# Moving the projection of k's second half ahead of a group of transposes in step 3

## The chip, the cores and the metric

The kernel runs on one core of one Trainium2 chip. The metric is the device time of one execution in microseconds (us). A time given below is the median of several runs; the profile is of one further execution.

## The reference

Attention over x [4, 1024, 128] with 16 heads of 64, then a layer norm, a feed-forward part with a token shift, and a second layer norm. Cut to what matters here:

```python
q = (x @ Wq).reshape(B, N, H, Dh).transpose(0, 2, 1, 3)      # B=4, N=1024, H=16, Dh=64
kv = x @ Wkv                                                 # k and v likewise
s = jnp.einsum('bhid,bhjd->bhij', q * scale, k)
gm = jnp.max(s, axis=-1, keepdims=True)
p = jnp.where(causal_mask, 0.0, jnp.exp(s - gm))
out = jnp.einsum('bhij,bhjd->bhid', p, v) / (jnp.sum(p, axis=-1, keepdims=True) + EPS)
x = _layernorm(x + (out.transpose(0, 2, 1, 3).reshape(B, N, H * Dh) @ Wo + bo))
x = _layernorm(x + ffn(x))
```

## The kernel before

The heads go through in 32 pairs `p` (4 batches of 8 pairs), two heads `a` = 0, 1 at a time. A pair has 8 steps `t`, one for each query tile of 128 rows. The order of the work on each engine is written out by hand, one loop over `p` and `t` for each engine (TensorE from L1114, ScalarE from L626, VectorE from L838, GpSimd from L434, the DMA queue of SyncE from L354); semaphores join them.

A query tile goes through the engines like this:

- TensorE, `scores(p, t)` (L974, its matmuls are recorded at L984): 12 matmuls fill two of three score buffers `ps_s`, one for each head. They wait until VectorE has emptied the buffers used before.
- VectorE, `evacuate(p, t, a)` (L746): scales a score buffer by -1/8 into an SBUF slot `tile` and takes the row minimum. For query tiles 4 to 7 VectorE also transposes blockwise (L755).
- GpSimd, `mask(p, t, a)` (L407): the diagonal block of 128x128.
- ScalarE, `exp_of(p, t, a)` (L576): the exponential over (t+1)*128 columns with its row sum.
- For query tiles 0 to 3 TensorE transposes the exponentials (`turn_tile`, L989, recorded at L997) one or more steps later, into a shared PSUM bank, and ScalarE copies them out to `pt` (`take_turned`, L610, recorded at L624). Tiles 2 and 3 are turned one head at a time, as `TURNED_IN` says: head 0 is part 0, head 1 is part 1.

Beside this TensorE does other work in each step: the projections of v (L927) and of the next pair's q and k (`qk_of`, L1001, recorded at L918; a projection is 3 matmuls of 512 columns, and ScalarE copies it out in `take_qk`, L579, recorded at L584, into `x1t` or `full`), the product with v (`values`, L1038), and the output projection (`project_out`, L1049). `QK` lists the four halves q 0, q 1, k 0, k 1; half n is projected in step n, so that k's second half is projected in step 3. GpSimd splits each half into a high and a low part (`split`, L391, recorded at L399 and L401) in step 0, 2, 4 or 5 (`SPLIT_AT`); that of k's second half is in step 5.

All this other work and the transposes share two PSUM banks, `ps_x`. `users_of_banks` (L81) lists the users of the banks in the order in which TensorE comes to them; user number n takes bank n % 2, and `drained` (L952) makes TensorE wait until ScalarE has emptied what user n - 2 had left in that bank.

`TURN_AT` says in which step which query tile is turned: tile 2 in step 3, tile 3 in step 4. `TURN_FIRST` lists the steps in which part 0 of the transposes stands directly behind the scores. In the other steps it stands behind the projections, together with the rest. The set is read in `users_of_banks`, in TensorE's loop and in ScalarE's loop:

```python
TURNED_IN = {0: ((0, 1),), 1: ((0, 1),), 2: ((0,), (1,)), 3: ((0,), (1,))}
TURN_AT = {1: 0, 2: 1, 3: 2, 4: 3}
TURN_FIRST = (1, 3, 4)
```

In the last pair, where no next pair is left to project, `turn_half` (L1060, recorded at L1066) and `take_sums` (L519, recorded at L522) take the place of `qk_of` and `take_qk`. Where a batch's x is turned for the next batch (pairs 1, 2, 9, 10, 17 and 18, `x_half`), step 1 has four more transposes and ScalarE two more copies.

Of the kernel before, what the change touches and what calls it, by code (L numbers as in the profile page):

```python
# [45 lines left out]
SPLIT_AT = {0: 0, 2: 1, 4: 2, 5: 3}  # L46
V_AT = {0: 0, 1: 1}
TURN_AT = {1: 0, 2: 1, 3: 2, 4: 3}
TURN_FIRST = (1, 3, 4)
X_AT = 1  # L50
OUT1_AT = 2
OUT0_AT = 4
# [28 lines left out]
def users_of_banks(p, t):  # L81
    users = []
    turned = [("quad", p, TURN_AT[t], n) for n in range(len(TURNED_IN[TURN_AT[t]]))
              ] if t in TURN_AT and p < ALL_PAIRS else []
    if t in TURN_FIRST:
        users += turned[0:1]
# [6 lines left out]
    if t == OUT1_AT and 1 < p:  # L93
        users.append(("out", p - 2, 1))
    users += turned[1:] if t in TURN_FIRST else turned
    if t == OUT0_AT and 0 < p <= ALL_PAIRS:
# [24 lines left out]
def build(nc, x, wq, wkv, wo, bo, w_r, w_k, w_v, mu_r, mu_k, out):  # L121
    r_dram = nc.dram_tensor("recips", [2, 2, N], F32).ap()

    with ExitStack() as ctx:  # L124
# [348 lines left out]
        def _(act):  # L473
# [121 lines left out]
            def take_values(p, k):  # L595

                c = min(k, 1)
                lo, hi = ((0, HALF), (HALF, HALF + 2 * P), (HALF + 2 * P, N))[k]
                act.wait_ge(s_pv[k], p + 1)

                at_least(act, s_yadd[c], p)
                act.activation(ot[:, lo:hi], ps_x[BANK["pv", p, k]][:, lo - c * HALF:hi - c * HALF], ACT.Copy
                               ).then_inc(s_ot[k], 1)

            def take_out(p, c):
                act.wait_ge(s_out, 2 * p + c + 1)
                act.activation(ot[:, c * HALF:(c + 1) * HALF], ps_x[BANK["out", p, c]][:, :], ACT.Copy  # L607
                               ).then_inc(s_outc, 1)

            def take_turned(p, t, n):  # L610
                heads = TURNED_IN[t][n]
                bank = ps_x[BANK["quad", p, t, n]][:, :]

                at_least(act, s_pv[0], p)
                act.wait_ge(s_quad, 8 * p + 2 * t + heads[-1] + 1)
                if t == 0:
                    act.activation(pt_unit(0).rearrange("p a (x c) -> p x a c", x=2)[:, :, :, 0:32],
                                   bank[:, 0:2 * P].rearrange("p (x a i) -> p x a i", x=2, a=4), ACT.Copy
                                   ).then_inc(s_pt, 1)
                    return  # L620
                for m, a in enumerate(heads):
                    cols = bank[:, m * (t + 1) * P:(m + 1) * (t + 1) * P].rearrange("p (j a i) -> p j a i", a=4, i=32)
                    place = pt_unit(t // 2)[:, :, place_of(t, a)].rearrange("p a (j i) -> p j a i", i=32)
                    act.activation(place, cols, ACT.Copy).then_inc(s_pt, 1)  # L624

            for p in range(ALL_PAIRS):  # L626
                for t in range(TILES):
# [4 lines left out]
                    if t == 7 and p > 0:  # L632
                        take_values(p - 1, 1)
                    if t in TURN_FIRST:
                        take_turned(p, TURN_AT[t], 0)
# [6 lines left out]
                    if t == OUT1_AT and p > 1:  # L642
                        take_out(p - 2, 1)
                    if t in TURN_AT and t not in TURN_FIRST:
                        take_turned(p, TURN_AT[t], 0)
# [263 lines left out]
        def _(pe):  # L909
# [64 lines left out]
            def scores(p, t):  # L974
                if t == 0 and p > 0:
                    pe.wait_ge(s_qklo, 4 * p)
                if p == 0 and t == 0:
                    pe.wait_ge(s_xy, 2)
                at_least(pe, s_evac, SLOTS * p + 2 * t + 2 - NSCORES)
                for c in range(2):  # L980
                    for m, (kh, qh) in enumerate(terms):
                        for a in range(2):
                            rows = slice(a * DH, (a + 1) * DH)
                            ins = mm(ps_s[scores_at(p, t, a)][:, c * HALF:(c + 1) * HALF], qs[rows, p % 2, qh, t * P:(t + 1) * P],  # L984
                                     ks[rows, p % 2, kh, c * HALF:(c + 1) * HALF], start=(m == 0), stop=(m == 2))
                            if c == 1 and m == 2:
                                ins.then_inc(s_scores, 1)

            def turn_tile(p, t, n):  # L989
                unit = ("quad", p, t, n)  # L990
                heads = TURNED_IN[t][n]
                drained(unit)
                for m, a in enumerate(heads):
                    pe.wait_ge(s_exp, SLOTS * p + 2 * t + a + 1)
                    for j in range(t + 1):
                        at = (m * (t + 1) + j) * P
                        ins = turn(ps_x[BANK[unit]][:, at:at + P], tile[:, slot_of(p, t, a), j * P:(j + 1) * P],  # L997
                                   ident[:, :])
                    ins.then_inc(s_quad, 1)
# [114 lines left out]
            for p in range(ALL_PAIRS):  # L1114
                for t in range(TILES):
                    scores(p, t)
                    if t in TURN_FIRST:
                        turn_tile(p, TURN_AT[t], 0)
# [8 lines left out]
                    if t in TURN_AT:  # L1127
                        for n in range(1 if t in TURN_FIRST else 0, len(TURNED_IN[TURN_AT[t]])):
                            turn_tile(p, TURN_AT[t], n)
# [75 lines left out]
```

## Time and profile before

| | |
|---|---|
| time, median of 3 runs | 1093.92 us (1092.81 to 1093.97) |
| the profiled execution's own time | 1094.0 us |
| its span, first to last instruction | 1092.0 us |
| TensorE busy | 1033.6 us (95%) |
| VectorE busy | 915.4 us (84%) |
| ScalarE busy | 746.6 us (68%) |
| GpSimd busy | 582.3 us (53%) |
| mean granted TensorE clock | 0.993 |

PE is TensorE's matmul row, PEld its weight loads, DVE is VectorE, ACT ScalarE, POOL GpSimd. Busy time of PE is of pipelined matmuls whose ends are modelled, so that one instruction can begin before the recorded end of the one before it. In a row of the timeline "x3" is three instructions merged, and "[0.31 <-ACT pt L624]" says that the engine was idle for 0.31 us before it and that the end of this wait came from ScalarE's instruction of line 624. ACT and DVE instructions also overlap a little: the next one begins about 0.1 us before the recorded end of the one before.

### The profile page before, as it was taken

The page shows a single profiled execution, that of the slowest core. Times are in us where ns is not written, and L with a number is a line of the kernel's source. Part 1 is how long each engine was busy: PE and PEld are TensorE (multiplying, and loading weights), DVE is VectorE, ACT ScalarE, POOL GpSimd, SP SyncE. Part 2 cuts the span into 40 slices and gives each one's busy share as a digit, 9 for nine tenths or more (in the row PEclk, how much of TensorE's full clock was granted, in tenths as well). Part 3 has the DMA queues.
Part 4 walks back from the last instruction along what each step waited for, and adds up shares of the span by engine and source line. Part 5 has one row for each costly group of instructions (what it writes and reads, how often), then busy time and mean ns, then how long its engine had stood idle before and what let it go on. Part 6 is the DMA issues. An engine that isn't in the chain of part 4 may idle for free. (4 is left out here: it accounts for less than half of the span.)

```text
span 1092.0 us, 22065 instructions
## 1 busy us (share of the span) xinstructions
PE 1033.6 (95%) x7427; PEld 673.6 (62%) x7427; DVE 915.4 (84%) x1546; ACT 746.6 (68%) x1709; POOL 582.3 (53%) x918
## 2 busy tenths in 40 slices
PE   7799999999999999999999999999999999999895
PEld 5565666666665666666666666666666666666563
DVE  5888888888887988888888888889888888898957
ACT  5766666666666666676666666666666766766767
POOL 5345655555564556566544556655555565554354
PEclk9999999999999999999999999999999999999998
DMA  5245555445555445555644455564445556554442
GB/s 162 69 111 123 136 141 123 117 111 125 134 124 136 118 109 122 131 123 136 146 113 106 114 134 123 139 145 118 115 114 126 132 126 146 123 124 117 115 106 77
DMA packets 74208, 134.05 MB, mean 123 GB/s; under 512 B 26864, under 2 KB 36848, under 8 KB 74096
## 3 DMA queue, kind: packets, MB, share of 16 engines
q1 hardware_dynamic: 73520, 132.26, 51.0%
q8 instruction: 59, 0.97, 0.4%
q10 hardware_dynamic: 576, 0.39, 0.1%
q14 instruction: 53, 0.43, 0.1%
HBM read 21.17 MB, written 2.36 MB: 22 GB/s over the span
## 5 line engine op out<-in xcount | busy, mean ns | idle before, releaser
L746 DVE TENSOR_SCALAR_CACHE_REDUCE tile<-ps_s 128x1024 f32<-128x1024 f32 x512 | 608.1, 1222 | 135.6 <-PE ps_s L984 128.0
L576 ACT ACTIVATE tile<-tile,neg_max 128x640 f32<-128x640 f32 (+7 forms) x512 | 396.2, 774 | 213.3 <-POOL tile L407 213.2
L984 PE MATMUL ps_s<-ks,qs 64*128 64x512 f32 x3072 | 424.2, 408 | 10.4 <-DVE tile L746 9.2
L407 POOL TENSOR_SCALAR_AFFINE_SELECT tile<-tile 128x128 f32<-128x128 f32 x512 | 149.7, 293 | 456.1 <-DVE tile L746 454.3
L984 PEld LDWEIGHTS ps_s<-ks,qs 64*128 64x128 f32 x3072 | 268.7, 184 | 129.3 <-issue 59.6
L1038 PE MATMUL ps_x<-pt,vs 128*64 128x256 f32 (+1 forms) x2560 | 270.2, 362 | 0.0
L755 DVE STREAM_TRANSPOSE stage<-tile 128x640 f32<-128x640 f32 (+3 forms) x256 | 255.2, 1026 | 0.0
L1038 PEld LDWEIGHTS ps_x<-pt,vs 128*64 128x64 f32 x2560 | 173.1, 137 | 109.3 <-issue 35.4
L997 PE MATMUL ps_x<-ident,tile 128*128 128x128 f32 x640 | 117.4, 290 | 26.5 <-ACT pt L624 15.8
L997 PEld LDWEIGHTS ps_x<-ident,tile 128*128 128x128 f32 x640 | 69.0, 140 | 107.0 <-issue 51.5
L918 PE MATMUL ps_x<-xs,ws 128*128 128x512 f32 x381 | 119.4, 423 | 0.6 <-DVE xs L721 0.4
L415 POOL TENSOR_TENSOR ot<-ot,rb 128x512 f32<-128x512 f32 x64 | 104.0, 1626 | 7.8 <-issue 5.2
L624 ACT ACTIVATE pt<-ps_x 128x256 f32<-128x256 f32 (+2 forms) x192 | 89.2, 483 | 12.3 <-PE ps_x L997 12.3
L576 ACT ACTIVATION_READ_ACCUMULATOR tile<-tile,neg_max 128x1 f32 x512 | 96.8, 189 | 0.0
L422 POOL TENSOR_TENSOR y<-y,ot 128x512 f32<-128x512 f32 x64 | 83.1, 1299 | 7.4 <-ACT ot L607 7.4
L401 POOL TENSOR_TENSOR qs<-x1t,qs 128x512 fp32r<-128x512 f32 x62 | 79.2, 1278 | 5.3
L591 ACT ACTIVATE vs<-ps_x 128x512 f32<-128x512 f32 x64 | 38.3, 598 | 56.5 <-PE ps_x L927 56.5
L918 PEld LDWEIGHTS ps_x<-xs,ws 128*128 128x128 f32 x381 | 63.5, 192 | 19.5 <-issue 11.3
L1049 PE MATMUL ps_x<-ot,wos 128*128 128x512 f32 x128 | 68.1, 613 | 2.8 <-POOL ot L415 2.4
L584 ACT ACTIVATE x1t<-ps_x 128x512 f32<-128x512 f32 x93 | 55.5, 597 | 9.3 <-PE ps_x L918 6.2
L927 PE MATMUL ps_x<-ws,xs 128*128 128x256 f32 x384 | 61.8, 296 | 0.0
L927 PEld LDWEIGHTS ps_x<-ws,xs 128*128 128x128 f32 x384 | 51.2, 193 | 11.5 <-issue 11.2
(92 smaller groups left out, 579.2 us busy)
## 6 DMA issues: line engine op xcount, KB each, us to landing
pt<-stage SPq DMA_DIRECT2D x512, 120.0 KB, 2.4
pt<-stage SPq DMA_DIRECT2D x512, 88.0 KB, 2.1
rb<-recips SPq DMA_DIRECT2D x64, 256.0 KB, 4.0
y<-in_L_attn_x SPq DMA_DIRECT2D x3, 512.0 KB, 8.7
out<-y SPq DMA_DIRECT2D x3, 512.0 KB, 3.2
pt<-in_L_attn_Wkv SPq DMA_DIRECT2D x2, 384.0 KB, 6.8
pt<-in_L_attn_x SPq DMA_DIRECT2D x2, 256.0 KB, 4.5
wos<-in_L_attn_Wo SPq DMA_DIRECT2D x1, 512.0 KB, 7.1
```

Source lines behind the costliest of these rows:

```text
L407: pool.affine_select(out=block_of, in_=block_of, compare_op=ALU.is_ge, fill=fill, base=0, pattern=[[-1, P]], channel_multiplier=1).then_in ...
L415: pool.tensor_tensor(cols, cols, rb[:, :].rearrange("p (i t) -> p t i", t=TILES)[:, 4 * c:4 * c + 4, :], ALU.mult).then_inc(s_norm[c], 1)
L422: pool.tensor_tensor(cols, cols, ot[:, c * HALF:(c + 1) * HALF], ALU.add).then_inc(s_yadd[c], 1)
L576: act.activation(cols, cols, ACT.Exp, bias=neg_max[:, at:at + 1], scale=-1.0, accum_out=sums[:, p % 2, a, t:t + 1]).then_inc(s_exp, 1)
L624: act.activation(place, cols, ACT.Copy).then_inc(s_pt, 1)
L746: dve.tensor_scalar(tile[:, at, :], ps_s[scores_at(p, t, a)][:, :], -SCALE, None, ALU.mult, ALU.min, accum_out=neg_max[:, at:at + 1]).then ...
L755: dve.transpose(stage_unit(u)[:, :, place_of(t, a)], tile[:, slot_of(p, t, a), 0:(t + 1) * P].rearrange("p (j b k) -> p b j k", b=4, k=32) ...
L918: ins = mm(bank, ws[:, "qk".index(what), wh, r * P:(r + 1) * P], xs[:, b % XSLOTS, xh, c * HALF:(c + 1) * HALF], start=(m == 0), stop=(m = ...
L927: ins = mm(bank[:, 2 * t * P:2 * (t + 1) * P], xs[:, b % XSLOTS, xh, at], ws[:, 2, wh, r * P:(r + 2) * P], start=(m == 0), stop=(m == 2))
L984: ins = mm(ps_s[scores_at(p, t, a)][:, c * HALF:(c + 1) * HALF], qs[rows, p % 2, qh, t * P:(t + 1) * P], ks[rows, p % 2, kh, c * HALF:(c + ...
L997: ins = turn(ps_x[BANK[unit]][:, at:at + P], tile[:, slot_of(p, t, a), j * P:(j + 1) * P], ident[:, :])
L1038: ins = mm(bank[a * DH:(a + 1) * DH, cols + (j == final) * P:cols + 2 * P], vs[:, v_place(p // 2, j), p % 2, a * DH:(a + 1) * DH], moving, ...
```

## The change

One entry of `TURN_FIRST` goes. It has three effects, all in step 3 of every pair:

- TensorE: the order scores, transposes of tile 2 head 0, projection of k's second half, transposes of tile 2 head 1 becomes scores, projection, transposes of head 0, transposes of head 1.
- ScalarE: `take_turned` of tile 2 head 0, `take_qk` of k's second half, `exp_of(p, 3, 0)` becomes `take_qk`, `take_turned`, `exp_of(p, 3, 0)`. The copy of head 1 stays between `exp_of(p, 3, 0)` and `exp_of(p, 3, 1)`.
- Banks: the three users of step 3 change places in the list, so that the projection gets the bank that head 0's transposes had, head 0's transposes get the other one, and head 1's transposes stay in their bank. That bank's user before them is now the projection; before the change it was head 0's transposes.

```diff
--- before.py
+++ after.py
@@ -46,7 +46,7 @@
 SPLIT_AT = {0: 0, 2: 1, 4: 2, 5: 3}
 V_AT = {0: 0, 1: 1}
 TURN_AT = {1: 0, 2: 1, 3: 2, 4: 3}
-TURN_FIRST = (1, 3, 4)
+TURN_FIRST = (1, 4)
 X_AT = 1
 OUT1_AT = 2
 OUT0_AT = 4
```

## Rows read from the trace of the kernel before

**Rows 1.** The page: busy time of TensorE, and the granted clock in 40 slices.

```profile
PE 1033.6 (95%) x7427; PEld 673.6 (62%) x7427; DVE 915.4 (84%) x1546; ACT 746.6 (68%) x1709; POOL 582.3 (53%) x918
PEclk9999999999999999999999999999999999999998
```

**Rows 2.** Waits of PE, 100 to 1000 us: total us, times, longest.

```profile
PE ps_x L997 <- ACT pt L624: 12.7, 28, 1.1
PE ps_x L997 <- ACT tile L576: 9.5, 28, 0.4
```

**Rows 3.** Timeline of PE in an ordinary pair: start us, us, engine line op.

```profile
404.91 0.96 PE L918 MATMUL ps_x<-xs,ws 128*128 128x512 f32 x3
...
405.71 1.02 PE L1049 MATMUL ps_x<-ot,wos 128*128 128x512 f32 x2
...
407.15 1.66 PE L984 MATMUL ps_s<-ks,qs 64*128 64x512 f32 x12
...
408.74 0.55 PE L997 MATMUL ps_x<-ident,tile 128*128 128x128 f32 x3
...
409.04 0.94 PE L918 MATMUL ps_x<-xs,ws 128*128 128x512 f32 x3
...
410.30 0.55 PE L997 MATMUL ps_x<-ident,tile 128*128 128x128 f32 x3 [0.31 <-ACT pt L624]
...
412.37 0.66 PE L997 MATMUL ps_x<-ident,tile 128*128 128x128 f32 x4
...
413.36 0.63 PE L997 MATMUL ps_x<-ident,tile 128*128 128x128 f32 x4 [0.33 <-ACT tile L576]
```

**Rows 4.** Timeline of ACT in the same pair.

```profile
407.32 0.66 ACT L624 ACTIVATE pt<-ps_x 128x256 f32<-128x256 f32 x2
...
409.16 0.62 ACT L576 ACTIVATE tile<-tile,neg_max 128x384 f32<-128x384 f32 x1 [0.59 <-POOL tile L407]
...
409.68 0.18 ACT L576 ACTIVATION_READ_ACCUMULATOR tile<-tile,neg_max 128x1 f32 x1
...
409.77 0.47 ACT L624 ACTIVATE pt<-ps_x 128x384 f32<-128x384 f32 x1
...
410.14 0.59 ACT L584 ACTIVATE x1t<-ps_x 128x512 f32<-128x512 f32 x1
...
411.32 0.73 ACT L576 ACTIVATE tile<-tile,neg_max 128x512 f32<-128x512 f32 x1 [0.58 <-POOL tile L407]
...
412.04 0.47 ACT L624 ACTIVATE pt<-ps_x 128x384 f32<-128x384 f32 x1
...
412.41 0.71 ACT L576 ACTIVATE tile<-tile,neg_max 128x512 f32<-128x512 f32 x1
```

**Rows 5.** Timeline of DVE and POOL in the same pair.

```profile
407.53 1.22 DVE L746 TENSOR_SCALAR_CACHE_REDUCE tile<-ps_s 128x1024 f32<-128x1024 f32 x1
...
409.77 1.27 POOL L401 TENSOR_TENSOR qs<-x1t,qs 128x512 fp32r<-128x512 f32 x1
...
410.99 0.69 POOL L407 TENSOR_SCALAR_AFFINE_SELECT tile<-tile 128x128 f32<-128x128 f32 x2
...
412.56 1.22 DVE L746 TENSOR_SCALAR_CACHE_REDUCE tile<-ps_s 128x1024 f32<-128x1024 f32 x1 [1.25 <-PE ps_s L984]
...
416.68 1.23 DVE L746 TENSOR_SCALAR_CACHE_REDUCE tile<-ps_s 128x1024 f32<-128x1024 f32 x1 [1.74 <-PE ps_s L984]
```

**Rows 6.** Timeline of PE in pair 0, a pair that turns x, and the last pair.

```profile
25.78 0.55 PE L997 MATMUL ps_x<-ident,tile 128*128 128x128 f32 x3
...
26.91 0.55 PE L997 MATMUL ps_x<-ident,tile 128*128 128x128 f32 x3
...
29.89 0.63 PE L997 MATMUL ps_x<-ident,tile 128*128 128x128 f32 x4 [0.26 <-ACT tile L576]
...
314.07 0.55 PE L997 MATMUL ps_x<-ident,tile 128*128 128x128 f32 x3 [1.07 <-ACT pt L624]
...
1011.66 0.55 PE L997 MATMUL ps_x<-ident,tile 128*128 128x128 f32 x3 [0.95 <-ACT pt L624]
```

## The prediction

> **What bounds the kernel now.** I read the page first. TensorE is busy for 95% of the span and its granted clock is full in nearly every slice [rows 1], so the question is where its remaining idle time lies and what closes each gap. The list of TensorE's waits answers: over 28 pairs nearly all its idle time is two waits a pair, both ahead of transposes [rows 2]. One ends with ScalarE's copy of line 624, 12.7 us in 28 waits; the other ends with an exponential, 9.5 us in 28 waits, or 0.34 us each, with a longest one of 0.4.
>
> The timeline of an ordinary pair, by engine, shows which these are. TensorE runs scores of step 3 at 407.15, head 0's transposes of tile 2 at 408.74, the projection at 409.04, and then stands still until 410.30, when head 1's transposes of tile 2 begin; scores of step 4 and head 0's transposes of tile 3 (412.37) follow; it stands still again until 413.36 [rows 3]. What the reader is to see is that TensorE is not what sets the second start. Followed back: head 1's transposes of tile 3 (413.36) need its exponential, begun at 412.41. That stood in ScalarE's queue behind the copy of 412.04, this behind the exponential of 411.32, and this waited for GpSimd's mask [rows 4]. The mask (410.99) came as soon as GpSimd was through with the subtraction of 409.77, which had begun behind the mask of tile 2 and so goes back to VectorE's pass of 407.53 [rows 5]. From the scores of step 2 to 413.36 the chain runs over VectorE, GpSimd and ScalarE, and the first gap of TensorE is slack within it. From 413.36 on TensorE is again the one that all wait for: VectorE stands idle for 1.74 us before it can begin step 5 [rows 5].
>
> **What the change removes.** The wait of head 1's transposes for the copy of head 0's goes, since they no longer follow each other in one bank. No instruction is added or taken away, no shape changes, and the moved work issues no DMA; it is moved past nothing on SyncE's queue or GpSimd's.
>
> **What it adds.** Head 1's transposes now wait for `take_qk` of the same step. I work out when each thing happens in the ordinary pair.
>
> 1. The projection starts where head 0's transposes did, at 408.74. Its bank was last used by an output projection, copied out before the copies of 407.32. Three projection matmuls hold TensorE for 405.71 - 404.91 = 0.80 us before the next group starts, and end after 0.96 us by the record [rows 3]. So it ends at 408.74 + 0.96 = 409.70.
> 2. Head 0's transposes start at 408.74 + 0.80 = 409.54. Their bank was emptied by the two copies of tile 1 (407.32 + 0.66 = 407.98), and ScalarE has begun head 1's exponential at 409.16, so head 0's is done [rows 4]. No new wait. They hold TensorE for 409.04 - 408.74 = 0.30 us, until 409.84, and end at 409.54 + 0.55 = 410.09 [rows 3].
> 3. ScalarE is free at 409.77, as before: that is when it began the copy behind the exponential [rows 4]. The projection is there since 409.70, so `take_qk` runs 409.77 to 410.36 (0.59 us). The copy of head 0's transposes follows after 0.5 us, 410.27 to 410.74, its input being ready at 410.09. Both together take ScalarE as long as in the old order, and both lie ahead of the exponential of 411.32, which has 0.58 us of idle time before it [rows 4].
> 4. Head 1's transposes start when `take_qk` is out. Before, the copy ended at 409.77 + 0.47 = 410.24 and they started at 410.30, 0.06 later [rows 3, 4]. Now it is 410.36 + 0.06 = 410.42. So the wait is not gone: it ends 0.59 - 0.47 = 0.12 us later.
> 5. Scores of step 4 and head 0's transposes of tile 3 slide by these 0.12 us, from 412.37 to 412.49. Head 1's of tile 3 have an idle time of 0.33 us before them [rows 3], and the exponential that ends it comes by a chain in which nothing has moved: VectorE's pass, GpSimd's mask and subtraction, ScalarE's exponential, the copy of head 1 (ready at 410.42 + 0.55 = 410.97, wanted at 412.04) and the next exponential [rows 4, 5]. The idle time shrinks to 0.21 us and the start stays at 413.36. VectorE begins step 4 (412.56) 0.12 us later and takes this out of the 1.74 us for which it waits before step 5 [rows 5].
>
> Sum for an ordinary pair: +0.12 us off the path, 0.00 on it. The six pairs that turn x have a first gap of 1.07 us, not 0.31 [rows 6], because the exponential is later; the difference of the two copies is the same 0.12 us, and the second gap is 0.34 there as elsewhere (28 waits, longest 0.4) [rows 2]. So zero too.
>
> Pair 0 is different: head 1's transposes did not wait there (26.91). Now they would start at 25.78 + 0.96 (projection) + 0.05 + 0.59 (copy) + 0.06 = 27.44, 0.53 us later, against a second gap of 0.26 us [rows 6]; some 0.3 us may remain of which the transposes' modelled ends hide a part. I take 0.1, with 0 and 0.5 as bounds, once. In the last pair a copy of sums takes the projection's place (wait of 0.95 us before the transposes [rows 6]); 0.12 us at most, once, and I take 0.
>
> Total: 31 x 0.00 + 0.1 = +0.1 us. The profiled execution took 1094.0 us (span 1092.0), 0.1 above the median of 1093.92, so I forecast 1094.0 us against that median.
>
> **A rule weighed.** The two groups of tile 2's transposes shared one bank before, and head 1's waited for head 0's copy [rows 3]; after the change they lie in different banks. The Trainium skill, Perfetto Trace Analysis, section Optimizing Tensor Performance, wants independent matmul groups rotated through different PSUM banks so that the evacuation of one overlaps the matmuls of the next; by that rule this order should be the better one and the first wait should go. By the sum above it doesn't go, since the bank that head 1's transposes get was filled just before by the projection, and the copy of that stands behind the same exponential.
>
> **The rivals.**
>
> - **The 0.12 us are paid in every pair (slower).** The place is the second gap. It decides once head 1's transposes of tile 2 come more than the 0.33 us later that the gap holds. My 0.12 leaves 0.21 spare, but step 3 above has ScalarE free only 0.07 us behind the projection's end: were the projection 0.3 us slower at the head of its new place than in step 2, the gap would be used up. If the slack were not there at all the price is 0.12 x 31 = 3.7 us, 1097.7 us. Against it: all 28 second gaps are alike (0.34 on average, longest 0.4) [rows 2], and each is an idle time recorded behind a modelled end, so the true slack is no smaller. 10%.
> - **The first wait really goes (faster).** This is the rotation rule as a mechanism: head 1's transposes start as soon as TensorE gets there (409.84) or its exponential is read out (409.68 + 0.18 = 409.86 [rows 4]), and the first gap closes. Were TensorE's own stream the bound throughout, that would be 31 gaps: 25 of some 0.33 and six of 1.07, about 14.7 us, or 1079.3 us. For it speaks that these are real idle times of the busiest engine. Against it: `take_qk` stands in the queue behind the same exponential, and even with the gap closed the chain over GpSimd sets 413.36. 3%.
> - **A small gain elsewhere (faster).** The projection is out 0.3 us earlier and its consumer, the split of step 5, could start earlier. It stands in GpSimd's queue at a time set by the masks of step 5, long after. At most what the second gap shows, if the exponential came earlier: 31 x 0.34 = 10.5 us, 1083.5 us; nothing moves it. 3%.
> - **Nothing changes on the path**, my forecast: 84%.
>
> **How the numbers follow.** 0.2% of 1093.9 is 2.2 us, about what a measurement of this kernel can tell from no change. The forecast (+0.1 with bounds 0 and +0.6 for pairs 0 and last) lies within it; so does half of the slower rival's span. The range reaches from 1092.4, the runs' own spread below the median, to 1096.0, up to which the slower rival is held in part. Faster 0.06, same 0.84, slower 0.10.
>
> **What the profile after would show.** Right: TensorE in step 3 has scores, L918, two groups of L997, and the wait of the second group ends with ScalarE's L584 and no longer L624. It is recorded from the modelled end of head 0's transposes (410.09), so it reads 410.42 - 410.09 = 0.33 us where it read 0.31. The wait for L576 shrinks from 0.34 to about 0.21 each; the time from one pair to the next stays as it was. Wrong, slower: the wait for L576 vanishes and the pair grows. Wrong, faster: no wait before the second group, and the exponential of step 3, head 1, earlier relative to the scores of step 2. The forecast also fails if ScalarE, GpSimd or VectorE have other durations once their neighbours in time move, which no row here prices.

## The result and the profile after

The changed kernel takes 1097.66 us (median of 5 runs, 1096.97 to 1098.53), the kernel before 1093.92 us beside it (5 runs, 1092.81 to 1094.25). The ratio is 1.004, with a 95% interval of 1.0029 to 1.0052. The change makes the kernel 0.4% slower. I had forecast no change and a range up to 1096.0.

The page of the changed kernel shows the same number of instructions and the same clock. TensorE's busy time is 6.6 us longer than in [rows 1] and ScalarE's 5.1 us, so the loss is recorded as work and not as waiting (the ends of matmuls are modelled, and the first experiment below, with the same order and a shorter copy, has 1034.8 us):

```profile
span 1096.5 us, 22065 instructions
PE 1040.2 (95%) x7427; PEld 678.6 (62%) x7427; DVE 914.0 (83%) x1546; ACT 751.7 (69%) x1709; POOL 582.3 (53%) x918
PEclk9999999999999999999999999999999999999998
```

TensorE's waits between 100 and 1000 us in the changed kernel, to be held against [rows 2]:

```profile
PE ps_x L997 <- ACT x1t L584: 14.1, 28, 1.1
PE ps_x L997 <- ACT tile L576: 6.4, 28, 0.2
```

Both lines are what the prediction had said. The first wait has not gone; it now ends with the copy of k's half (L584). The second has shrunk from 0.34 us each to 6.4 / 28 = 0.23. By this list TensorE waits less in all than before (20.5 us against 22.2), and yet the kernel is slower.

From pair 1 on the loss comes evenly. Here is the start of head 1's transposes of tile 3 in pairs 1 and 30 (PE's timeline), first in the kernel before:

```profile
61.54 0.63 PE L997 MATMUL ps_x<-ident,tile 128*128 128x128 f32 x4 [0.35 <-ACT tile L576]
...
983.52 0.63 PE L997 MATMUL ps_x<-ident,tile 128*128 128x128 f32 x4 [0.34 <-ACT tile L576]
```

and in the changed one:

```profile
62.27 0.63 PE L997 MATMUL ps_x<-ident,tile 128*128 128x128 f32 x4 [0.23 <-ACT tile L576]
...
988.00 0.63 PE L997 MATMUL ps_x<-ident,tile 128*128 128x128 f32 x4 [0.24 <-ACT tile L576]
```

The distance grows from 0.73 to 4.48 us: 3.75 us in 29 pairs, 0.13 us a pair. That is the size of the 0.12 us that I had worked out for the later start and then called hidden. The 0.73 us that are there in pair 1 are looked at below.

An ordinary pair of the changed kernel, TensorE (PE) and its weight loads (PEld), from the scores of step 3 on, answers to [rows 3]:

```profile
409.30 1.66 PE L984 MATMUL ps_s<-ks,qs 64*128 64x512 f32 x12
...
410.89 0.98 PE L918 MATMUL ps_x<-xs,ws 128*128 128x512 f32 x3
...
411.71 0.49 PE L997 MATMUL ps_x<-ident,tile 128*128 128x128 f32 x3
...
412.56 0.55 PE L997 MATMUL ps_x<-ident,tile 128*128 128x128 f32 x3 [0.36 <-ACT x1t L584]
...
414.63 0.66 PE L997 MATMUL ps_x<-ident,tile 128*128 128x128 f32 x4
...
415.51 0.63 PE L997 MATMUL ps_x<-ident,tile 128*128 128x128 f32 x4 [0.22 <-ACT tile L576]
...
416.10 0.30 PEld L1049 LDWEIGHTS ps_x<-ot,wos 128*128 128x128 f32 x2 [0.20 <-issue]
416.13 1.10 PE L1049 MATMUL ps_x<-ot,wos 128*128 128x512 f32 x2
```

and its ScalarE, which answers to [rows 4]:

```profile
411.92 0.59 ACT L584 ACTIVATE x1t<-ps_x 128x512 f32<-128x512 f32 x1
...
412.40 0.49 ACT L624 ACTIVATE pt<-ps_x 128x384 f32<-128x384 f32 x1
...
415.18 0.19 ACT L576 ACTIVATION_READ_ACCUMULATOR tile<-tile,neg_max 128x1 f32 x1
...
415.38 0.60 ACT L624 ACTIVATE pt<-ps_x 128x512 f32<-128x512 f32 x1
```

The same place in the kernel before, with rows that stand in no group so far:

```profile
413.02 0.19 ACT L576 ACTIVATION_READ_ACCUMULATOR tile<-tile,neg_max 128x1 f32 x1
413.12 0.60 ACT L624 ACTIVATE pt<-ps_x 128x512 f32<-128x512 f32 x1
...
413.83 0.30 PEld L1049 LDWEIGHTS ps_x<-ot,wos 128*128 128x128 f32 x2
413.87 1.10 PE L1049 MATMUL ps_x<-ot,wos 128*128 128x512 f32 x2
```

Counted from the start of the scores of step 3 (407.15 and 409.30):

| | before | after |
|---|---|---|
| head 1's transposes of tile 2 start | 3.15 | 3.26 |
| head 0's transposes of tile 3 start, end | 5.22, 5.88 | 5.33, 5.99 |
| head 1's transposes of tile 3 start | 6.21 | 6.21 |
| ScalarE's copy of head 0's (L624) starts, ends | 5.97, 6.57 | 6.08, 6.68 |
| output projection: weight load starts | 6.68 | 6.80 |

The third row is the one that I had taken for the end of the matter: it has not moved. The instruction behind it has. The output projection (L1049) lies in the bank in which head 0's transposes of tile 3 lie, and waits for their copy. That copy started 0.09 us after the recorded end of the transposes in both kernels, so it went along with them, and the weight load followed 0.11 to 0.12 us behind the copy in both.

Pair 0 has no output projection in step 4, and pays more, once. The scores of steps 3 and 5 and VectorE's first pass of step 4 in the kernel before:

```profile
24.20 1.65 PE L984 MATMUL ps_s<-ks,qs 64*128 64x512 f32 x12
...
29.17 1.22 DVE L746 TENSOR_SCALAR_CACHE_REDUCE tile<-ps_s 128x1024 f32<-128x1024 f32 x1 [0.81 <-PE ps_s L984]
...
30.46 1.66 PE L984 MATMUL ps_s<-ks,qs 64*128 64x512 f32 x12
```

and in the changed one, with head 1's transposes of tile 2:

```profile
24.28 1.66 PE L984 MATMUL ps_s<-ks,qs 64*128 64x512 f32 x12
...
27.52 0.55 PE L997 MATMUL ps_x<-ident,tile 128*128 128x128 f32 x3 [0.36 <-ACT x1t L584]
...
29.79 1.23 DVE L746 TENSOR_SCALAR_CACHE_REDUCE tile<-ps_s 128x1024 f32<-128x1024 f32 x1 [1.35 <-PE ps_s L984]
...
31.07 1.66 PE L984 MATMUL ps_s<-ks,qs 64*128 64x512 f32 x12 [0.39 <-DVE tile L746]
```

Step 3 begins 0.08 us later in the changed kernel. Counted from there, head 1's transposes start at 3.24 us in place of 2.71 (26.91 in [rows 6]), 0.53 later, and the scores of step 5 at 6.79 in place of 6.26, again 0.53 later. They stand 0.05 to 0.07 us behind the end of VectorE's pass in both kernels: in this pair the whole delay goes on over VectorE. With the 0.08 us this is 0.61 of the 0.73 us by which the traces differ in pair 1; the other 0.12 come up between 42 and 51 us, and what they are stays open. So the price is about 0.5 us for pair 0 and 0.12 us for each of the 31 others.

### The profile page after: what moved, and what is told of

The parts are those of the page before. It is cut to its first block and busy times, and to the rows that moved or that the text cites. A ratio compares the mean times of both kernels' runs of the same rounds, so it can differ in the third digit from the quotient of the medians.

```text
span 1096.5 us, 22065 instructions
## 1 busy us (share of the span) xinstructions
PE 1040.2 (95%) x7427; PEld 678.6 (62%) x7427; DVE 914.0 (83%) x1546; ACT 751.7 (69%) x1709; POOL 582.3 (53%) x918
## 5 line engine op out<-in xcount | busy, mean ns | idle before, releaser
L1038 PE MATMUL ps_x<-pt,vs 128*64 128x256 f32 (+1 forms) x2560 | 270.2, 362 | 0.0
L1038 PEld LDWEIGHTS ps_x<-pt,vs 128*64 128x64 f32 x2560 | 173.0, 137 | 109.4 <-issue 35.5
L997 PEld LDWEIGHTS ps_x<-ident,tile 128*128 128x128 f32 x640 | 71.5, 140 | 92.7 <-issue 37.1
L624 ACT ACTIVATE pt<-ps_x 128x256 f32<-128x256 f32 (+2 forms) x192 | 89.9, 487 | 9.5 <-PE ps_x L997 9.1
L1049 PE MATMUL ps_x<-ot,wos 128*128 128x512 f32 x128 | 67.9, 612 | 2.7 <-POOL ot L415 2.3
L584 ACT ACTIVATE x1t<-ps_x 128x512 f32<-128x512 f32 x93 | 55.4, 596 | 9.5 <-PE ps_x L918 6.4
```

The source lines that it names most:

```text
L1038: ins = mm(bank[a * DH:(a + 1) * DH, cols + (j == final) * P:cols + 2 * P], vs[:, v_place(p // 2, j), p % 2, a * DH:(a + 1) * DH], moving, ...
```

## The experiments

All were run beside the kernel before on the same chip; each ratio is against it. For each trace I also give the length of a pair that turns x (from one start of the 32 matmuls of L1038 in step 7 to the next, median of five): 33.39 us before, 33.52 after. The other pairs are shorter (31.43 and 31.56) and differ by as much. Theory A is the chain over the bank. Theory B is that the order costs TensorE itself something. Theory C is that the delay reaches the path another way than over that bank.

### Undo the longer copy, keep the new order

```diff
-                act.activation(full[n], ps_x[BANK["qk", p, n]][:, :], ACT.Copy).then_inc(s_full, 1)
+                cols = 384 if n == 3 else HALF
+                act.activation(full[n][:, 0:cols], ps_x[BANK["qk", p, n]][:, 0:cols], ACT.Copy).then_inc(s_full, 1)
```

> The changed kernel, with ScalarE copying only 384 of the 512 columns of k's second half out of PSUM (128 columns of k are left stale), so that this copy is as short as the 384-column copy for which head 1's transposes waited before. Theory A (a chain over a bank): the longer copy makes head 1's transposes of tile 2 start 0.12 us later, this makes head 0's transposes of tile 3 end 0.12 us later, ScalarE's copy of those too, and the output projection of step 4, whose bank that copy empties, starts later by as much in every pair. Then the 0.12 us go and the time is that of the kernel before, 1093.9 (+-0.7). Theory B (order on TensorE): to have the projection between the scores and the transposes costs TensorE itself something, by weight loads or by the switch of shapes. Then the time stays at 1097.7.

Measured: 1093.89 us against 1092.84, ratio 1.0008 (0.9999 to 1.0017); pair 33.40 us. From pair 1 on the loss is gone, though TensorE still has the new order and the new banks. Theory B falls: what the change costs there is the length of the copy that head 1's transposes wait for. In pair 0 the product with v still comes 8.28 us after the scores of step 3 (24.48 and 32.76), 0.44 later than before: there head 1's transposes did not wait at all, and now they wait until the projection is done and copied, however short the copy.

### Shorten the copy that empties the output projection's bank

```diff
+                    few = 3 if p > 0 and (t, n) == (3, 0) else t + 1
-                    act.activation(place, cols, ACT.Copy).then_inc(s_pt, 1)
+                    act.activation(place[:, 0:few], cols[:, 0:few], ACT.Copy).then_inc(s_pt, 1)
```

> The changed kernel, with ScalarE copying only three of the four blocks of head 0's transposes of tile 3 in step 4 (one block of the transposed exponentials is left stale from pair 1 on), which ends that copy about 0.12 us sooner. Theory A: the output projection gets its bank 0.12 us sooner and the whole loss comes back: 1093.9 to 1094.5. Theory B: the time stays near 1097.7. A third theory C (the 0.12 us reach the path over the exponential of step 3 or over VectorE, not over the bank): stays near 1097.7 too, while the short copy of k would still recover it.

Measured: 1094.3 us against 1092.84, ratio 1.001 (1.0001 to 1.0019); pair 33.40 us. Most of the loss is back, by an edit that leaves everything up to the transposes of tile 3 as in the changed kernel. It begins with pair 1, so the 0.5 us of pair 0 stay. Its rows of step 4:

```profile
413.49 0.65 PE L998 MATMUL ps_x<-ident,tile 128*128 128x128 f32 x4
...
414.24 0.49 ACT L625 ACTIVATE pt<-ps_x 128x384 f32<-128x384 f32 x1
...
414.84 0.30 PEld L1050 LDWEIGHTS ps_x<-ot,wos 128*128 128x128 f32 x2
```

The copy still starts late (0.10 us behind the transposes' end), ends at 414.73 thanks to its shorter length, and the weight load comes 0.11 us behind it.

### The same in the kernel before

The same edit on the kernel before.

> The kernel before, with the same shortened copy of head 0's transposes of tile 3. In the trace of before TensorE starts the output projection 0.51 us after head 1's transposes, as close as four transposes allow (0.49 us elsewhere), so the copy and TensorE's own stream end almost together. Theory A: at most 0.02 to 0.05 us a pair to gain, 1092.3 to 1093.9. If instead the bank is a wait of its own size in the kernel before too, the gain would be near 0.12 us a pair, 1090.2.

Measured: 1089.49 us against 1092.84, ratio 0.9971 (0.996 to 0.9981); pair 33.28 us. My expectation was a miss: 0.11 us a pair came back, not 0.02 to 0.05. So the kernel before was already waiting for that bank in every pair. Its rows:

```profile
412.49 0.49 ACT L625 ACTIVATE pt<-ps_x 128x384 f32<-128x384 f32 x1
...
413.10 0.30 PEld L1050 LDWEIGHTS ps_x<-ot,wos 128*128 128x128 f32 x2
```

The weight load again comes 0.12 us behind the copy's end (412.98). Held against the run above, which has the same short copy, the change of step 3 still costs 0.12 us a pair (33.40 against 33.28): both wait for that copy, and with the new order it starts later by what its transposes come later. In the kernel before, the wait stands in no list, because the four transposes ahead of the projection are recorded until 413.36 + 0.63 = 413.99, after the projection has begun. The Trainium skill, Perfetto Trace Analysis, Tensor Engine Instruction, says that TensorE's recorded ends are estimated from size and delay and not observed; this case agrees, with a wait of 0.1 us beneath a recorded overlap.

### Delay the copy in the kernel before, with no change of order

```diff
             for p in range(ALL_PAIRS):
                 for t in range(TILES):
+                    if t == 3:
+                        act.activation(pad_to[:, :], bo_col[:, :], ACT.Copy)
```

> The kernel before with one more ScalarE instruction in each pair, a copy of one column between SBUF tiles, right ahead of the copy of head 0's transposes of tile 2. TensorE's order, the banks and everything else stay as before. By the nearest rows (the accumulator read holds ScalarE for 0.09 us net, an 8-column activation for about 0.2) it delays that copy by 0.1 to 0.25 us. Theory A: this delay alone does what the change did, 31 x 0.1 to 0.25 = 3 to 8 us slower, 1097 to 1102. Theory B: the time stays at 1093.9, for nothing of TensorE's order has changed.

Measured: 1095.7 us against 1092.84, ratio 1.0025 (1.0016 to 1.0034); pair 33.49 us. The rows:

```profile
410.96 0.19 ACT L630 ACTIVATE pad_to<-bo_col 128x1 f32<-128x1 f32 x1
411.06 0.47 ACT L625 ACTIVATE pt<-ps_x 128x384 f32<-128x384 f32 x1
```

The copy starts 0.10 us later than it would have, and the pair is 0.10 us longer. The time lies below the 1097 to 1102 that I had expected, since the kernel beside it took 1092.84 and the delay was the least of those that I had allowed for; 2.9 us against 31 x 0.10 = 3.1 fits. The old order with a later copy does what the change did, in the same proportion.

### Is it a slope or a point?

The changed kernel with 256 columns (the first diff with `cols = 256`), and the changed kernel with the added instruction of the last diff.

> The changed kernel, with ScalarE copying only 256 of the 512 columns of k's second half (half of it is left stale), so that head 1's transposes of tile 2 can start some 0.1 us earlier than in the kernel before. Theory A, refined by the rows so far: in the kernel before, ScalarE is free for the copy of head 0's transposes of tile 3 at the same moment, to 0.01 us, at which their result is there. A delay costs one for one and an advance gains nothing: the time is that of the run with 384 columns, 1093.9, and not 3 us below it. Rival D: the time is proportional on both sides, and this run comes to about 1090.5.

> The changed kernel with the one-column ScalarE copy in front of the copy of k's second half, the instruction that cost the kernel before 2.7 us (0.10 us a pair at its place). Theory A: past the point at which ScalarE and the transposes meet, every delay counts in full: 0.10 x 31 = 3.1 us more than the changed kernel, 1100 to 1101. A rival in which 0.12 us is a step of its own (another order of waiting, once) and not a slope: about 1098.

Measured: 1093.11 us against 1093.13 with 256 columns, ratio 0.9996 (0.9987 to 1.0005), pair 33.39; 1099.45 us against 1093.43 with the added instruction, ratio 1.0052 (1.004 to 1.0064), pair 33.59. The second lies a little under the 1100 to 1101 that I had expected. The first kernel starts head 1's transposes of tile 2 at 3.04 us, 0.11 earlier than before (410.71 - 407.67), and its rows show why nothing is gained:

```profile
412.81 0.63 PE L998 MATMUL ps_x<-ident,tile 128*128 128x128 f32 x4
...
413.55 0.19 ACT L576 ACTIVATION_READ_ACCUMULATOR tile<-tile,neg_max 128x1 f32 x1
413.64 0.59 ACT L625 ACTIVATE pt<-ps_x 128x512 f32<-128x512 f32 x1
```

The transposes end at 413.44, 0.20 us before the copy starts, and what it waits for is ScalarE's own exponential. Earlier is worth nothing, later costs in full up to nearly twice the delay of the change: 33.39, 33.52 and 33.59 us a pair for a start of head 1's transposes of tile 2 that is 0, 0.11 and 0.20 us later than before. The kernel before stands at the bend, to 0.01 us (an instruction begins 0.09 to 0.10 us ahead of the recorded end of a readout, so ScalarE is free at 413.02 + 0.19 - 0.09 = 413.12, or 5.97 after the scores; the transposes' result is there at 5.88 + 0.09 = 5.97).

### Take the output projection away from the bank

First out of step 4, with `OUT0_AT = 5` in place of 4, in both kernels. The bank is the same there, but its copy has long been out when the projection comes.

> The changed kernel with the output projection of the previous pair moved from step 4 to step 5, behind the scores. It no longer stands behind the copy that empties its bank. Theory A: the change of order in step 3 then costs nothing, and this run and its twin (the kernel before with the same move) have the same time within 1 us; both about 1091 to 1093, since TensorE keeps the same work and loses only a few hundredths of a us at the seams. Theory B or C: this run is 3 to 4 us slower than its twin.

> The kernel before with the output projection of the previous pair moved from step 4 to step 5: the twin of the run above. Theory A: same time as that, about 1091 to 1093. Theory B or C: 3 to 4 us faster than that.

Measured: 1097.25 us on the changed kernel (1.0033, 1.002 to 1.0046), 1095.86 us on the kernel before (1.0023, 1.0014 to 1.0032), against 1093.13; pairs 33.52 and 33.48 us. The difference of the twins fell from 3.7 us to 1.4, but not to the 1 us or less that I had expected, and both are slower than the kernel before, where I had expected 1091 to 1093. The rows of the changed kernel with the move:

```profile
415.20 1.22 DVE L746 TENSOR_SCALAR_CACHE_REDUCE tile<-ps_s 128x1024 f32<-128x1024 f32 x1 [1.36 <-PE ps_s L984]
...
416.49 1.22 PEld L984 LDWEIGHTS ps_s<-ks,qs 64*128 64x128 f32 x12 [0.21 <-DVE tile L746]
```

With the projection gone, the scores of step 5 stand directly behind the transposes, and these need a third score buffer, which VectorE empties in its first pass of step 4. That pass starts when the scores of step 4 are done, so it too is 0.1 us later in the changed kernel: a second way for the same delay, the one of pair 0. It costs here what it delays the scores of step 5 by, 6.80 us after those of step 3 against 6.77 in the twin. The output projection covers it in its old place (there the scores of step 5 come 1 us later). Why the twin is 2.7 us slower than the kernel before stays open: from the start of head 1's transposes of tile 3 to the product with v (L1038) it takes 3.20 us where that takes 3.12.

Then between the two groups of transposes of tile 3, in both kernels, on TensorE, ScalarE and in the order of banks:

```diff
+    if t == OUT0_AT and 0 < p <= ALL_PAIRS:
+        users.append(("out", p - 1, 0))
     users += turned[1:] if t in TURN_FIRST else turned
-    if t == OUT0_AT and 0 < p <= ALL_PAIRS:
-        users.append(("out", p - 1, 0))
...
+                    if t == OUT0_AT and 0 < p:
+                        take_out(p - 1, 0)
                     if t == 4:
                         take_turned(p, TURN_AT[t], 1)
                     exp_of(p, t, 0)
...
-                    if t == OUT0_AT and 0 < p:
-                        take_out(p - 1, 0)
                     exp_of(p, t, 1)
...
+                    if t == OUT0_AT and 0 < p:
+                        project_out(p - 1, 0)
                     if t in TURN_AT:
                         for n in range(1 if t in TURN_FIRST else 0, len(TURNED_IN[TURN_AT[t]])):
                             turn_tile(p, TURN_AT[t], n)
-                    if t == OUT0_AT and 0 < p:
-                        project_out(p - 1, 0)
```

> The kernel before with the output projection of step 4 put between the two groups of transposes of tile 3, on TensorE, on ScalarE (its copy ahead of head 1's) and in the order of the banks. It fills TensorE's wait for the exponential of head 1. Its bank is then that which the copy of tile 2 head 1 empties, which is done 0.8 us before; head 1's transposes wait for the copy of head 0's instead, some 0.47 us later than now, but scores of step 5 follow them directly. Theory A: 0.4 to 0.48 us a pair gained, 1079 to 1082. Rival: ScalarE, which now has to copy two things in turn before the exponential of step 4, delays that by about 0.9 us and eats the gain: 1090 or more.

> The changed kernel with the output projection of step 4 between the two groups of transposes of tile 3, the same move as in the run of the kernel before that took 1088.7 us. There the projection no longer waits for the copy of head 0's transposes but for GpSimd's product that is its operand, at 6.14 us after the scores of step 3; head 1's transposes start behind it at 7.10, and their bank is free from 6.67. With the 0.12 us that the change adds the bank would be free at 6.79, still 0.3 ahead of 7.10. Theory A: here the change of step 3 costs nothing, 1088.7 (+-1). Theory C (the 0.12 us reach the path another way than over that bank): 1092.4, which is 3.7 more.

Measured: 1088.68 us on the kernel before (0.9955, 0.9941 to 0.9969, against 1093.13), 1090.31 us on the changed one (0.9971, 0.996 to 0.9983, against 1093.43); pairs 33.17 and 33.18 us. Of the 12 to 15 us that I had expected on the kernel before only 4.4 came: the output projection now waits for GpSimd's product, its operand, first in the kernel before with the move and then in the changed one with it:

```profile
412.18 1.13 PE L1049 MATMUL ps_x<-ot,wos 128*128 128x512 f32 x2 [0.28 <-POOL ot L415]
```

```profile
411.15 1.57 POOL L415 TENSOR_TENSOR ot<-ot,rb 128x512 f32<-128x512 f32 x1 [0.32 <-DMA rb<-recips]
...
412.77 1.13 PE L1049 MATMUL ps_x<-ot,wos 128*128 128x512 f32 x2 [0.46 <-POOL ot L415]
```

The exponentials of step 4 do start 0.9 us later, as the rival of that expectation had it (8.29 us after the scores of step 3, before 7.43), but TensorE's list of waits has none for them.

But the move serves the question. Where the output projection no longer waits for the copy of head 0's transposes, the change of step 3 costs 0.01 us a pair in place of 0.12 (0.02 in the pairs that do not turn x). Over the medians 1.6 us are left, with intervals that overlap, and 1090.31 lies above the 1088.7 (+-1) that I had expected. Pair 0 has 0.5 of them: its product with v comes 8.37 us after the scores of step 3 against 7.85 in the twin. From the first to the last start of the 32 matmuls, which leaves pair 0 out, the two traces differ by 0.8 us. Whether this rest is the change, or the product's wait for a transfer (0.32 us in the pair above, the only such wait listed between 100 and 1000 us), I have not separated.

The kernel before with the projection in between is faster than both kernels of the study.

## Why the prediction was wrong

- **The bound.** That TensorE's two listed waits are a slack within a chain over VectorE, GpSimd and ScalarE was right: head 1's transposes of tile 3 start at 6.21 us with either order. That "TensorE is again the one that all wait for" from there on was wrong: the next instruction waits for ScalarE's copy of head 0's transposes.
- **Steps 1 to 4** held to 0.02 us, but for the recorded end of head 0's transposes (2.94 forecast, 2.90 found). The others, counted from the scores of step 3: projection end 2.55 forecast and 1.59 + 0.98 = 2.57 found, `take_qk` at 2.62, head 1's transposes at 3.27 forecast and 3.26 found, the wait passed on and not removed. The Trainium skill's rule on rotating banks (Perfetto Trace Analysis, Optimizing Tensor Performance) would have had the wait go; the two groups now lie in different banks and the wait reads 0.36 us where it read 0.31. The bank is free of the one copy and full of another.
- **Step 5 is the one that failed.** I followed the 0.12 us through "scores of step 4 and head 0's transposes of tile 3" to head 1's transposes, found 0.33 us of idle time there, and stopped. Head 0's transposes have a reader of their own, the copy, which in the kernel before was due at the very moment at which they ended, and the output projection takes their bank. I had followed the order of the banks for the three users in step 3 and not for those of step 4. The term is 0.12 us x 31 = 3.7 us where I had put 0.
- **The slower rival** had the price of a pair and the wrong place. It was to decide only when the 0.33 us were used up; 0.23 us of them are still there. That its 1097.7 meets the measured 1097.66 is in part luck: it leaves out the 0.5 us of pair 0, with which the sum is 4.2 us, where the medians differ by 3.7 (3.2 to 5.7 by the interval) and the two profiled spans by 4.5.
- **Pair 0** was mis-sized: 0.1 us forecast, with 0.5 as the upper bound, and 0.53 found. The later start of head 1's transposes was right (0.53 forecast and found). Wrong was that the second gap would take part of it: the delay goes over VectorE's first pass of step 4, directly behind which the scores of step 5 start in this pair. The sum had looked at the second gap alone.
- **What I held to be slack** in the kernel before, the run with the shorter copy shows to be a wait of about 0.11 us a pair, unlisted.

## What to carry to other kernels

When a group slides by a little, follow every reader of its result and every later user of its bank, not just the next instruction on the same engine; idle time before one instruction says nothing of the one behind it. Look at the first pass of a loop by itself: another engine can be the bound there. On TensorE a wait can lie beneath a recorded overlap: compare when its weight load starts with when the copy that frees its bank ends. A distance that stays the same (here 0.11 to 0.12 us) while edits move the copy is a wait; in a single trace it could be chance. Where two things meet to 0.01 us, a delay costs one for one and an advance brings nothing.

## What the runs showed of the hardware

ScalarE's copy out of PSUM took 0.58 to 0.60 us for 512 columns, 0.47 to 0.49 for 384 and 0.36 to 0.39 for 256, so some 0.11 to 0.12 us for 128 columns. A copy of a single column is recorded with 0.19 us and held the next instruction up by 0.10. From the end of the copy of head 0's transposes of tile 3 to the weight load of the output projection passed 0.11 to 0.12 us, but only 0.05 us from the end of the copy that head 1's transposes of tile 2 wait for to theirs (411.92 + 0.59 = 412.51, weight load at 412.56 in the changed kernel); what makes the difference no run shows. From the recorded end of four transposes to the copy that waits for them passed 0.09 to 0.10 us.
